# A quantised feed-forward that works by blocks of 512 tokens, with its weights and its norm prepared inside the attention ahead

## The reference

```python
    x = x + _L3_xattn_ref(_layernorm(x, axis=-1), ctx_1024, ctx_1024, fside_BxS2_0, L3_xattn_wq, ...)
    x = x + _L3_ffn_ref(_layernorm(x, axis=-1), L3_ffn_clip_x, L3_ffn_clip_down, L3_ffn_w_gate, L3_ffn_w_up, L3_ffn_w_down)

def _act_fake_quant(x, clip_factor):
    scale = jax.nn.sigmoid(clip_factor) * jnp.max(jnp.abs(x)) / QMAX
    return jnp.clip(_ste_round(x / scale), -QMAX - 1.0, QMAX) * scale

def _weight_fake_quant(w):
    scale = jnp.max(jnp.abs(w), axis=1, keepdims=True) / QMAX
    return jnp.clip(_ste_round(w / scale), -QMAX - 1.0, QMAX) * scale

xq = _act_fake_quant(x, clip_x[0])
gate = jnp.einsum('bsh,ih->bsi', xq, _weight_fake_quant(w_gate))
up = jnp.einsum('bsh,ih->bsi', xq, _weight_fake_quant(w_up))
h = _act_fake_quant(jax.nn.silu(gate) * up, clip_down[0])
return jnp.einsum('bsi,hi->bsh', h, _weight_fake_quant(w_down))
```

## Time and profile before

| quantity | value |
|---|---|
| median of 3 runs | 1918.81 us (1916.26 to 1918.91) |
| profiled execution | 1919.11 us |
| its span | 1917.3 us |
[...]
| busy: PE, DVE, ACT, POOL | 85%, 67%, 56%, 28% |

### The profile page before, as it was taken

The page is one execution under the profiler, slowest core; times in us unless marked ns, Lnnn a source line. Parts: engine busy times, 40 slices in busy tenths (PEclk is TensorE's granted clock), DMA queues, the critical chain, the costliest instruction groups (busy, mean ns, idle before and its releaser), DMA issues. The chain is left out here.

```text
span 1917.3 us, 32972 instructions
## 1 busy us (share of the span) xinstructions
PE 1634.2 (85%) x11001; PEld 872.8 (46%) x11001; DVE 1277.2 (67%) x3390; ACT 1068.4 (56%) x2316; POOL 544.6 (28%) x615
## 2 busy tenths in 40 slices
PE   6868999984499999999999889979799778999933
PEld 4522333332255555555555456655566542333311
DVE  5546666736766666666666878856788566777656
ACT  3313666657555545555555468854688523766723
POOL 0316454301100000000000178814688213433000
PEclk9886999997699999999999999999899985999966
DMA  5214333101100000000000000001200003222000
GB/s 153 45 36 113 76 69 72 38 2 56 35 1 6 5 2 7 2 5 24 1 1 1 1 7 1 0 11 34 44 1 0 9 13 72 40 45 50 6 12 22
DMA packets 60189, 53.44 MB, mean 28 GB/s; under 512 B 9562, under 2 KB 52750, under 8 KB 59926
## 3 DMA queue, kind: packets, MB, share of 16 engines
q1 hardware_dynamic: 59190, 51.30, 11.4%
q10 hardware_dynamic: 864, 0.39, 0.1%
HBM read 30.57 MB, written 1.05 MB: 16 GB/s over the span
## 5 line engine op out<-in xcount | busy, mean ns | idle before, releaser
L1629 DVE CUSTOM_DVE_ANT_0 minus_s_l2x<-s_ps_l2x,mask_b_l2x 128x512 f32<-128x512 f32 x256 | 166.6, 689 | 181.8 <-PE s_ps_l2x L1845 181.7
L1754 ACT ACTIVATE probs_l2x<-minus_s_l2x,nmax_l2x 128x512 f32<-128x512 f32 x256 | 182.7, 714 | 187.2 <-DVE nmax_l2x L1629 187.1
L1047 DVE CUSTOM_DVE_ANT_0 junk_l1x<-s_ps_l1x,mask_b_l1x 128x512 f32<-128x512 f32 x256 | 166.4, 688 | 78.9 <-PE s_ps_l1x L1233 77.4
L1050 DVE TENSOR_REDUCE nmax_l3x<-s_ps_l3x 128x1 f32<-128x512 f32 x256 | 163.5, 685 | 55.5 <-PE s_ps_l3x L1233 53.6
L1099 ACT ACTIVATE pT_l1x<-st_ps_l1x 128x1024 f32<-128x1024 f32 x128 | 131.1, 1025 | 72.7 <-PE st_ps_l1x L1219 72.2
L1702 DVE COPY pT_l2x<-t_ps_l2x 128x512 f32<-128x512 f32 x256 | 164.3, 683 | 0.5 <-PE t_ps_l2x L1854 0.5
L1854 PEld LDWEIGHTS t_ps_l2x<-consts,probs_l2x 128*128 128x128 f32 x1024 | 109.6, 141 | 98.7 <-issue 87.2
L1854 PE MATMUL t_ps_l2x<-consts,probs_l2x 128*128 128x128 f32 x1024 | 139.8, 279 | 1.9 <-ACT probs_l2x L1754 1.9
L2285 POOL TENSOR_TENSOR rn_l2a_first<-ssc_l2a_first,consts 128x16 f32<-128x16 f32 x28 | 107.3, 3833 | 33.5 <-DVE ssc_l2a_first L2312 32.6
L2455 ACT ACTIVATE probs_l2a<-minus_s_l2a,nmax_l2a 128x128 f32<-128x128 f32 (+1 forms) x256 | 105.9, 417 | 10.3 <-DVE nmax_l2a L2360 9.0
L2241 POOL TENSOR_TENSOR v_l2x_first<-kT_l2x_first,tb_l2a_first 128x256 f32<-128x256 f32 x112 | 97.8, 900 | 13.2 <-ACT kT_l2x_first L2423 12.3
(11 more groups left out here) (528 smaller groups left out, 3629.8 us busy)
## 6 DMA issues: line engine op xcount, KB each, us to landing
...
ctxT_l0x<-in_ctxT SPq DMA_DIRECT2D x9, 256.0 KB, 3.2
rows_l0x<-in_ctx SPq DMA_DIRECT2D x9, 256.0 KB, 4.2
```

What stands on the lines that cost most here:

```text
L1047: dve.tensor_tensor_reduce(out=junk[w][:], in0=s_ps[w][:], in1=mask_b[b % 2][:, j, :], scale=-1.0, scalar=3e38, op0=ALU.add, op1=ALU.min, ...
L1050: dve.tensor_reduce(to, s_ps[w][:], AX.X, ALU.max, negate=True).then_inc(m.s_drained[w].sem, 1)
L1629: dve.tensor_tensor_reduce(out=minus_s[n % 4][:], in0=s_ps[n % 2][:], in1=mask_b[b % 2][:], scale=-1.0, scalar=3e38, op0=ALU.add, op1=ALU. ...
L1754: act.activation(probs[n % 4][:], minus_s[n % 4][:], ACT.Exp, bias=nmax[:, b % 2, n:n + 1], scale=-1.0, accum_out=sums[:, b % 2, j, h:h + ...
```

## The change

A class `FirstQuant` takes over the first part of the feed-forward and is handed to the layer 3 attention as `follow`. SP issues the nine loads after the attention's third context load. DVE computes the moments of batch b's final x at half slot 28+16b (2t+j in the code) and its scaled norm and largest absolute value at 34+16b, for the first seven batches, and for the last one behind the attention's last residual add; POOL's power for batch b has the key 8b+15. The weights are rounded in four parts at half slots 36, 38, 40 and 42. Scratch space is taken from buffers that already exist. In the feed-forward, `find_scale(0)` reads 8 peaks instead of 2048 values, rounding and turning go by blocks of 512 tokens, `hT` is laid out by block, each block's peak is taken after its product, all loops are written out, ACT loads Silu's table before the first gate and zeroes the padding of `hT` (32x4x512, on DVE before), and SP stores each 512-token block once its x is added. The phase `store` is gone.

```diff
                 load_ctx(2)
+                if follow is not None:
+                    follow.load(sp)
                 for b in range(2, B):
...
+                if follow is not None:
+                    order += [(8 * b + 15, follow.power, (pool, b)) for b in range(B)]
                 for _, step, args in sorted(order, key=lambda s: s[0]):
                     step(*args)
...
+                        if follow is not None:
+                            at, slot = divmod(2 * t + j - FOLLOWED, 16)
+                            if slot == 0 and 0 <= at < B - 1:
+                                dve.wait_ge(*is_drained(OUT, at, 0))
+                                follow.moments(dve, at)
+                            if slot == 6 and 0 <= at < B - 1:
+                                follow.scale(dve, at)
+                            if at == 0 and slot in range(8, 8 + 2 * follow.PARTS, 2):
+                                follow.weights(dve, slot // 2 - 4)
                 dve.wait_ge(*m.misc_drained.after(len(jobs)))
+                if follow is not None:
+                    follow.moments(dve, B - 1)
+                    follow.scale(dve, B - 1)
+                    follow.finish(dve)
+    def load(self, sp):
+        m, d = self.m, self.m.dram
+        sp.dma_start(self.wd, d["L3_ffn_w_down"]).then_inc(m.quant_loaded.sem, 16)
+        for n, name in enumerate(("L3_ffn_clip_x", "L3_ffn_clip_down")):
+            sp.dma_start(self.clips[:, n:n + 1], d[name][0, :].partition_broadcast(P)).then_inc(m.quant_loaded.sem, 16)
+        for n, name in enumerate(("L3_ffn_w_gate", "L3_ffn_w_up")):
+            for c, r in enumerate(self.ROWS):
+                sp.dma_start(self.w[0:r, n, c, :], d[name][c * P:c * P + r, :]).then_inc(m.quant_loaded.sem, 16)
+        self.loads = 16 * (3 + 2 * self.NC)
...
+    def moments(self, dve, b):
+        m, x = self.m, self.m.x
+        tiles = range(TPB * b, TPB * (b + 1))
+        for t in tiles:
+            dve.bn_stats(self.st[:, t, :], x[:, t, :]).then_inc(m.out_stats.sem, 1)
+        dve.wait_ge(*m.out_stats.after(TPB * (b + 1)))
+        for t in tiles:
+            dve.bn_aggr(self.mv[:, t, :], self.st[:, t, :]).then_inc(m.out_moments.sem, 1)
+        dve.wait_ge(*m.out_moments.after(TPB * (b + 1)))
+        cols = slice(TPB * b, TPB * (b + 1))
+        dve.tensor_scalar(self.ve[:, cols], self.mv[:, cols, 1], LN_EPS, None, ALU.add).then_inc(m.out_eps.sem, 1)
...
+    def power(self, pool, b):
+        m, cols = self.m, slice(TPB * b, TPB * (b + 1))
+        pool.wait_ge(*m.out_eps.after(b + 1))
+        pool.tensor_tensor(self.rs[:, cols], self.ve[:, cols], m.consts["minus_half"][:, 0:TPB], ALU.pow).then_inc(m.out_rstd.sem, 1)
+    def scale(self, dve, b):
+        m, x, cols = self.m, self.m.x, slice(TPB * b, TPB * (b + 1))
+        dve.wait_ge(*m.out_rstd.after(b + 1))
+        for t in range(TPB * b, TPB * (b + 1)):
+            dve.tensor_scalar(self.xn[:, t, :], x[:, t, :], self.mv[:, t, 0:1], self.rs[:, t:t + 1], ALU.subtract, ALU.mult)\
+                .then_inc(m.out_normed.sem, 1)
+        dve.wait_ge(*m.out_normed.after(TPB * (b + 1)))
+        dve.tensor_reduce(self.peaks[:, b:b + 1], self.xn[:, cols, :].rearrange("p t d -> p (t d)"), AX.X, ALU.max,
+                          apply_absolute_value=True).then_inc(m.out_peaked.sem, 1)
...
+                tokens = m.out.rearrange("(t p) d -> p t d", p=P)
+                for n in range(NB):
+                    tiles = slice(TB * n, TB * (n + 1))
+                    sp.wait_ge(*m.x_updated.after(n + 1))
+                    sp.dma_start(tokens[:, tiles, :], x[:, tiles, :]).then_inc(m.loaded.sem, 16)
...
+                def quantise(n):
+                    rows = slice(TB * n, TB * (n + 1))
+                    flat = xn[:, rows, :].rearrange("p t d -> p (t d)")
+                    at = 2 + 2 * n
+                    dve.tensor_scalar(flat, flat, inv[:, 0:1], -QMAX - 1, ALU.mult, ALU.max).then_inc(m.step.sem, 1)
+                    dve.wait_ge(*m.step.after(at + 1))
+                    dve.tensor_scalar(flat, flat, QMAX, MAGIC, ALU.min, ALU.add).then_inc(m.step.sem, 1)
+                    dve.wait_ge(*m.step.after(at + 2))
+                    dve.tensor_scalar(xq[:, rows, :].rearrange("p t d -> p (t d)"), flat, MAGIC, None, ALU.subtract).then_inc(m.x_quantised.sem, 1)
...
+                def hidden(n):
                     for c, r in enumerate(ROWS):
                         dve.wait_ge(*m.gate_ready.after(NC * n + c + 1))
...
+                        dve.scalar_tensor_tensor(out=hT[0:r, n, c, :], in0=u_ps[c][0:r, :], scalar=hscale[0:r, 1, c:c + 1],
+                                                 in1=gate[c][0:r, :], op0=ALU.mult, op1=ALU.mult).then_inc(m.hidden_ready.sem, 1)
+                def block_peak(n):
+                    dve.wait_ge(*m.hidden_ready.after(NC * (n + 1)))
+                    dve.tensor_reduce(tops[:, n:n + 1], hT[:, n].rearrange("p c t -> p (c t)"), AX.X, ALU.max, apply_absolute_value=True)\
+                        .then_inc(m.hidden_clipped.sem, 1)
+                def round_hidden(n):
+                    h = hT[:, n].rearrange("p c t -> p (c t)")
+                    dve.tensor_scalar(h, h, inv[:, 1:2], -QMAX - 1, ALU.mult, ALU.max).then_inc(m.hidden_clipped.sem, 1)
+                    dve.wait_ge(*m.hidden_clipped.after(NB + n + 1))
+                    dve.tensor_scalar(h, h, QMAX, MAGIC, ALU.min, ALU.add).then_inc(m.hidden_rounded.sem, 1)
+                def add_output(n):
...
+                find_scale(0, quant.peaks, 0)
+                dve.tensor_scalar(hscale[:], wscale, scale[:, 0:1], None, ALU.mult).then_inc(m.scales_ready.sem, 1)
+                quantise(0)
+                quantise(1)
+                dve.wait_ge(*m.scales_ready.after(1))
+                dve.wait_ge(*m.zeroed.after(1))
+                for n in range(NB):
+                    hidden(n)
+                    if n + 2 < NB:
+                        quantise(n + 2)
+                    block_peak(n)
+                dve.wait_ge(*m.hidden_clipped.after(NB))
+                find_scale(1, tops[:], SCALED)
                 dve.tensor_scalar(dB[:], d_bank[:, 0:D], scale[:, 1:2], None, ALU.mult).then_inc(m.step.sem, 1)
...
+                for n in range(NB - 1):
+                    round_hidden(n)
+                dve.wait_ge(*m.step.after(SCALED + 3))
+                add_output(0)
+                round_hidden(NB - 1)
+                for n in range(1, NB):
+                    add_output(n)
...
-                act.wait_ge(*m.loaded.after(16 * (3 + 2 * NC)))
-                act.activation(sig[:], clips[:], ACT.Sigmoid).then_inc(m.act_step.sem, 1)
+                act.activation(sig[:], quant.clips, ACT.Sigmoid).then_inc(m.act_step.sem, 1)
+                act.activation(hT[LAST:P, :, NC - 1, :], k["ones"][LAST:P, 0:1].unsqueeze(1).to_broadcast([P - LAST, NB, BT]), ACT.Copy, scale=0.0)\
+                    .then_inc(m.zeroed.sem, 1)
...
+                act.activation(warm[:], quant.clips, ACT.Silu).then_inc(m.act_step.sem, 1)
+                def copy_turned(n):
                     act.wait_ge(*m.x_turned.after(n + 1))
-                    act.activation(xqT[:, n * T // 2:(n + 1) * T // 2], x_banks[n][:].bitcast(BF16), ACT.Copy)\
+                    act.activation(xqT[:, n * BT:(n + 1) * BT], y_ps[n % 2][:, 0:BT // 2].bitcast(BF16), ACT.Copy)\
                         .then_inc(m.turned_copied.sem, 1)
...
+                copy_turned(0)
+                copy_turned(1)
                 act.wait_ge(*m.scales_ready.after(1))
-                with act.Fori(0, NB) as n:
+                for n in range(NB):
                     for c, r in enumerate(ROWS):
                         act.wait_ge(*m.scores_ready.after(NC * n + c + 1))
+                        if n:
+                            act.wait_ge(*m.hidden_ready.after(NC * (n - 1) + c + 1))
                         act.activation(gate[c][0:r, :], g_ps[c][0:r, :], ACT.Silu, scale=hscale[0:r, 0, c:c + 1])\
                             .then_inc(m.gate_ready.sem, 1)
-                with act.Fori(0, NB) as n:
+                    if n + 2 < NB:
+                        copy_turned(n + 2)
+                for n in range(NB):
                     act.wait_ge(*m.hidden_rounded.after(n + 1))
-                    act.activation(hq[:, :, bass.ds(n * BT, BT)], hT[:, :, bass.ds(n * BT, BT)], ACT.Copy, bias=-MAGIC)\
+                    act.activation(hq[:, n].rearrange("p c t -> p (c t)"), hT[:, n].rearrange("p c t -> p (c t)"), ACT.Copy, bias=-MAGIC)\
                         .then_inc(m.hidden_quantised.sem, 1)
...
+                turn(0)
+                turn(1)
+                for n in range(NB):
+                    pe.wait_ge(*m.turned_copied.after(3 + n + 1))
                     for c, r in enumerate(ROWS):
-                        if c == 0:
-                            pe.wait_ge(*m.hidden_ready.after(NC * n))
```

(12 more changed lines are left out.)

254 lines of the change are left out of this document (123 added, 131 removed).

## The result

The changed kernel takes 1896.28 us in the median (1891.4 to 1899.07, 4 runs), the kernel before 1917.53 (1916.05 to 1918.91, 4 runs). The ratio is 0.9891 with a 95% interval of 0.9876 to 0.9905, so the change makes the kernel 21.2 us faster; 1897 was forecast. The profiled execution has a span of 1894.6 us, 22.7 less than before, with a mean granted clock of 0.927 of the full one, before 0.923.

A forecast was written before the change was run, and what follows sets the result against it. PE was taken to set the attention's pace, DVE to end nearly everything behind it. 80.1 us there become 52.4, 27.7 less; the attention pays 5.8: 1919.1 - 27.7 + 5.8 = 1897.2, so 1897, range 1892 to 1902.

The forecast's parts named there:

- the last norm: Behind the attention's last residual add: the last batch's scaled norm, 2.4 us, plus its peak, 0.4, together 2.9 us.
- the boundary: Between the attention's block and the feed-forward's: ACT starts 0.5 us after the add, taken as 0.6 us.
- up to the end of the first copy: Feed-forward start until the first turned tokens are copied: ACT's list of table loads, zeroing and copies ends last, 6.7 us.
- the hidden blocks: Feed-forward products, roundings and peaks by block: spacings 6.3, 5.9, 3.9, last block 3.7, 2.3 ahead; 22.1 us.
- the store: End of the span: the last quarter's store, 256 KB, takes 3.0 us; the first three lie beside work.
- Step 6: Rounding and output at the feed-forward's end: 17.26 us less 2.1 for cheaper passes and 0.3 for loops, 14.8 us.
- for the four batches in which both run: Attention: scale passes beside POOL's splits are occasionally stretched; 1.0 us added for four batches.
- The prediction's own sign of being wrong: Steady attention batches growing by more than a us each would show the prediction wrong.
- every scale pass is stretched: Rival, attention: two passes in each of four batches go from 344 to 729 ns, 3.1 us, so 1899; chance 0.12.
- The weights: Attention: rounding the weights in four parts, 4.9 us of work, costs 0.5 + 0 + 1.3 + 1.3, so 3.1 us.
- The moments: Attention: 1.0 us of work per batch, free for batches 0 to 3, 0.7 each for batches 4 and 5.
- the first rival: Attention takes all inserts in full, 16.9 us in place of 5.8, giving 1908; chance 0.10.

The follow-up runs named there:

- experiment 4: Changed kernel with POOL instead of ACT zeroing the padding of `hT`: 1893.09 us, stage behind the last add 50.1, attention 274.8.
- experiment 6: Changed kernel with one DMA storing all of x after the last add instead of a store per block: 1899.22 us, stage behind the last add 53.4.
- experiment 5: Changed kernel with `hT` in its old chunk-by-chunk layout, each block three runs of 512: 1904.78 us, stage behind the last add 52.2.
- 8: Changed kernel with PE's turn and ACT's copy one block ahead instead of two: 1895.53 us, stage behind the last add 48.5, attention 274.8.
- experiment 1: Changed kernel with each batch's scale two half slots later (36+16b), where POOL is done with its splits: 1895.29 us, attention 270.5.
- 2: Changed kernel with the scale at 37+16b (slot 9), beside DMA traffic but without POOL work: 1890.87 us, attention 269.8.
- the two with all moves: Changed kernel with later scales, weights behind the last maxima, POOL zeroing and later turn: 1889.3 us; the second, weights directly behind batch 6's scale: 1882.38 us.
- 3: Changed kernel with the four parts of the weights' rounding behind batch 6's scale, after the last maxima: 1894.51 us, attention 271.2.
- experiment 7: Changed kernel with all batches' moments, powers and scales behind the attention's last add, weights left in it: 1897.01 us, attention 269.9.

## Why the prediction came out right, and which of its steps did not

**The stage behind the last add** was summed to 52.4 us and measured 50.7. Step by step, forecast and trace: the last norm 2.9 and 2.9; the boundary 0.6 and 0.5; up to the end of the first copy 6.7 and 6.6, with ACT's list late as written (experiment 4 shows both that it was and why taking 1.9 us from it gives only 0.6); the hidden blocks 22.1 and 21.9; `find_scale(1)` 2.3 and 2.4; the store 3.0 and 2.8 (experiment 6).

That the hidden blocks fit is in part luck, since errors cancel. The spacing of 6.3 us was 0.2 more than its own terms add up to, the first product came 2.0 us behind the copy and not 2.3, the first hole was 0.6 and not 0.9, and against that the products behind the holes took 2.45 us for three instead of the sum's 2.1.

Step 6, rounding and output, was mis-sized: 14.8 foretold, 13.6 measured (1878.24 to 1891.83), which is 3.7 less than before. The passes are as foretold, 1.01 and 0.96 us, and experiment 5 shows that the layout makes them so; they give 2.1. The other terms are read from the two traces, and no run tests them one by one. Without the loop the add starts 0.72 us after its scaling (L3127 to L3131) where it was 0.87 (L3047 to L3051), 0.6 for four blocks; the sum had 0.3 for the loops. And VectorE loses 0.5 us to PE between the outputs instead of 1.5, which the sum left out: the first output now lies between the third and the fourth rounding, while ACT and PE work on the third block.

One run of 1536 costs 1.01 us and three runs of 512 cost 1.27, the latter as much as 2048 in one run, 1.28. Why three runs cost that much no run shows.

**The attention** is where the prediction failed, with 5.8 us foretold and 11.7 measured. The step was the 1.0 us "for the four batches in which both run", with the clock taken as it was. The prediction's own sign of being wrong, steady batches that grow by more than a us each, came true: the two batches behind the weights grew from 28.6 to 30.7 us. Four experiments (4, 5, 6 and 8) left the attention as it is in the changed kernel, and theirs took 274.8, 278.3, 277.4 and 274.8 us. So the price of one execution lies between 9.2 and 12.6 us against the one profile of the kernel before, and 5.8 is outside in all five.

- The scale beside POOL: 0.1 per batch and 1.0 for all of the contention were foretold. The passes went from 0.34 to 0.78 and 0.83 us, and each of the four half slots grew by 0.89 us, 3.5 in all. A row of the other attention, where one instruction in sixteen was stretched to 729 ns, was taken as the rate at which it happens. In the trace two passes of one batch are stretched there (541 and 729 ns, from 138.96 on), beside POOL's mask instruction L951, and six of the eight batches have no POOL work beside these passes at all. So the row gave no rate for a pass beside POOL, and here both passes stand in the half slot in which POOL works without a pause. The rival "every scale pass is stretched" was the true one, and at a higher price than its 0.39 us per pass. Experiments 1 and 2 show the cause: away from the splits a pass takes 0.34 us, beside them 0.78 or 0.83. POOL's splits take 0.67 to 0.73 us with a scale beside them and without one in experiment 1. How POOL's work stretches the pass no run shows. One place in the trace before doesn't fit and stays open: at 162.04 two such passes took 0.34 us each beside the same mask instruction L951 (160.68 to 164.31).
- The falls of the clock: none was foretold. Four cost 4.6 us here. Twelve profiles are to hand. The kernel before, the one with the scale at slot 9 and the two with all moves show none. The others show one to four, each close behind a scale or a part of the weights: four in the changed kernel and in experiment 6, three in 5, two in 3, 4 and 8, one in 1 and 7. All six profiles with the scales at the place of the changed kernel have one to three falls behind a scale. In the six others no fall stands behind a scale, but for the one of experiment 1, whose half slot holds a scale and a part of the weights. So the falls go with these inserts. That PE's wait for VectorE is what brings them is only likely, and the stretch isn't needed for one, as batch 4 shows. Which insert brings a fall varies between executions and stays open, and so does the price, 0.9 to 1.3 us here and up to 2.3 in experiment 7.
- The weights: 3.1 foretold, 2.4 measured in the half slots that hold them. The moments: 1.4 foretold for batches 4 and 5, 0.8 measured, and nothing for the others, as foretold.
- The scale of batch 4, without splits beside it: 0.4 and 0.4. The items make 3.5 + 4.6 + 2.4 + 0.8 + 0.4 = 11.7 us.

**The forecast of 1897 against 1896.28** therefore owes something to chance. By the lengths of the two stretches the change is worth 17.6 us and the kernel should take about 1900; the medians say 21.2. The 3.6 us between them I put down to the part ahead of the attention, in which nothing was changed, which scatters by 9 us and was 5.1 us shorter in the profile after. By 1900 the forecast would still have been inside its range of 1892 to 1902, so it is the closeness that was luck. So was the last add "near 1843 instead of 1837": it ended at 1843.87, as 11.7 us more in the attention and 5.1 less ahead of it. What sets that part's length in one execution was not found: its mean granted clock, from 0 to 1563, is 0.94 in three of the twelve profiles and 0.95 in nine, and whether that is cause or effect was not tested.

POOL's power came early enough wherever maxima stood behind it (VectorE waited for it in the last two batches alone, 0.8 us each), SP's nine loads delayed nothing that was waited for, and the first rival, all inserts in full, did not happen: 16.9 us were its price and 11.7 were paid. This was nearer to it than to the forecast's 5.8, though for another reason.
